# A decoder block on one NeuronCore: linear attention in chunks of 64 tokens, two to a tile, in smaller tiles of TensorE's array, with TensorE's step in another order

## The reference

```
h = layernorm(x);  q, k, v = split(h @ qkv_w.T + qkv_b)      # 16 heads of 16
q = relu(q) + 1e-6;  k = relu(k) + 1e-6
kv    = cumsum over tokens of (k outer v)                     # causal
num   = q . kv
den   = max(q . cumsum(k), 1e-6)
x     = x + (num / den) @ out_w.T + out_b
```

## Time and profile before

| | |
|---|---|
| runs | 379.93, 380.64, 380.88 us; median 380.64 |
| span of the profiled execution, first to last instruction | 377.9 us |
| TensorE busy | 356.6 us, 94% of the span |
| VectorE | 296.1 us, 78% |
| GpSimd | 279.1 us, 74% |
| ScalarE | 162.6 us, 43% |
| granted clock of TensorE, mean | 0.988 |
| the loop's score products, first and last | 31.0 and 271 us |

### The profile page before, as it was taken

How to read it: one execution, slowest core, us unless ns; L and a number is a source line. 1 busy time by engine, 2 the same in 40 slices (tenths; PEclk the granted TensorE clock), 3 DMA queues, 4 the chain that set the end, 5 groups by cost and what they waited for, 6 DMA issues and landing times. The chain is left out here.

```text
span 377.9 us, 10670 instructions
## 1 busy us (share of the span) xinstructions
PE 356.6 (94%) x3514; PEld 255.6 (68%) x3514; DVE 296.1 (78%) x922; ACT 162.6 (43%) x394; POOL 279.1 (74%) x414
## 2 busy tenths in 40 slices
PE   8999999999999999999999999999899989998781
PEld 4566677777677777767777777778676556655451
DVE  2588788898989898888898878886756588799462
ACT  2463553454455346436436524442456435331120
POOL 5338987766777866877867789898978888578455
PEclk9999999999999999999999999999999999999897
DMA  8993881200300120032121013003000233148750
GB/s 255 328 308 88 251 245 22 66 16 16 72 31 16 35 53 16 19 83 87 55 49 39 25 25 67 16 20 80 16 31 28 73 97 111 57 146 283 220 181 23
DMA packets 39309, 34.50 MB, mean 91 GB/s; under 512 B 4505, under 2 KB 38456, under 8 KB 39256
## 3 DMA queue, kind: packets, MB, share of 16 engines
q1 hardware_dynamic: 36392, 29.54, 27.7%
q0 software_dynamic: 1312, 3.37, 2.9%
q10 hardware_dynamic: 1552, 0.92, 0.9%
HBM read 17.55 MB, written 12.60 MB: 80 GB/s over the span
## 5 line engine op out<-in xcount | busy, mean ns | idle before, releaser
L1650 POOL TENSOR_TENSOR s_t<-s_t,causal 128x512 f32<-128x512 f32 x63 | 78.9, 1273 | 15.6 <-ACT s_t L961 15.4
L539 PE MATMUL bank<-h1t,w_qkv 128*128 128x512 f32 x112 | 52.9, 595 | 0.4 <-DVE x L1220 0.3
L1207 DVE TENSOR_TENSOR s_t<-sbank,causal 128x512 f32<-128x512 f32 x65 | 43.5, 671 | 1.1 <-PE sbank L560 1.0
L1642 POOL TENSOR_TENSOR state_wide<-state,own_pair 128x256 f32<-128x256 f32 x28 | 18.9, 676 | 25.5 <-DVE state L1198 24.4
L961 ACT ACTIVATE s_t<-sbank 128x512 f32<-128x512 f32 x63 | 33.7, 587 | 7.8 <-PE sbank L560 7.8
L560 PE MATMUL sbank<-arena 32*128 32x256 f32 x512 | 36.7, 400 | 0.0
L599 PE MATMUL bank<-s_t,vp 128*32 128x128 f32 x1024 | 34.6, 275 | 1.1 <-DVE s_t L1207 0.4
L546 PE MATMUL bank<-w_qkv,h1t 128*128 128x256 f32 x128 | 34.2, 389 | 0.0
L1658 POOL TENSOR_TENSOR rr<-ve,neg_half 128x3 f32<-128x3 f32 x36 | 31.9, 887 | 3.0
L684 PE MATMUL bank<-w_out,attn_t 128*128 128x256 f32 x128 | 33.6, 385 | 0.5 <-DVE attn_t L1288 0.5
L778 PE MATMUL sbank<-h1t,w 128*128 128x512 f32 x72 | 33.0, 596 | 0.5 <-ACT h1t L961 0.5
(11 more groups left out here) (231 smaller groups left out, 831.5 us busy)
## 6 DMA issues: line engine op xcount, KB each, us to landing
rden_t<-rden SPq DMA_DIRECT2D x64, 64.0 KB
rows<-x SPq DMA_DIRECT2D x32, 128.0 KB, 1.7
x<-in_x SPq DMA_DIRECT2D x7, 512.0 KB, 8.6
out<-x SPq DMA_DIRECT2D x7, 512.0 KB
we<-in_we SPq DMA_DIRECT2D x1, 2048.0 KB
xmask<-in_mask POOLq DMA_DIRECT2D x2, 616.0 KB, 10.3
rows<-empty SPq DMA_DIRECT2D x1, 1032.0 KB, 5.2
we<-in_we SPq DMA_DIRECT2D x1, 1024.0 KB
```

The costliest lines, as they stand in the source:

```text
L539: mm = pe.matmul(dst[:, :], w_qkv[:, ch, cb * P:(cb + 1) * P], h1t[:, g % 3, ch, :], start=(ch == 0), stop=(ch == CH - 1))
L1207: dve.tensor_tensor(s_t[:, r, :, :], sbank[r][:, :].rearrange("p (s q) -> p s q", s=4), causal[:, :].unsqueeze(1).to_broadcast([P, 4, P]), ...
L1650: pool.tensor_tensor(s_t[:, r, :, :], s_t[:, r, :, :], causal[:, :].unsqueeze(1).to_broadcast([P, 4, P]), ALU.mult)\
```

## The change

A tile now holds two chunks of 64 tokens. The scores of a chunk against itself are 64 by 64: for each of 2 channel blocks, 2 chunks and 4 head pairs one product in an array tile of 32 rows by 64 columns (16 products for 8). The numerators are products of 64 keys by 64 queries in tiles of 64 rows by 32 columns (32 for 16), into columns of sbank2 and 3 that the scores no longer use. There is a state per chunk: `inner_state` ahead of the tile's second chunk, `next_state` ahead of the next tile. `from_state` multiplies 64 queries of each chunk by its own state (16 products for 2, in column tiles of 32; 8 in a batch's first tile, which had none). The sums of keys by values are made per chunk (16 for 8), into sbank2 and 3. The masks are of 64 columns, and the whole score data is half as large: ScalarE copies it once, VectorE and GpSimd mask once each. The spread state is twice as large. s_t has two halves used in turn in the same room. `be_rest`, `over`, `past` and `block_oh` of the later expert stage share room with the spread state, which is no longer used then.

TensorE's step is reordered: transposes, q/k block, cross scores, from_state, numerators, sums, transposes of h1(F), values, denominators (now into bank 3), scores, and the rest as it was. The scores wait for more: `attn_ready` and all states of the tile. VectorE evicts the values and converts the mask later in its step, the attention product and the states come before the scan or query product, and the reciprocal of the softmax's sum stands between the two states. ScalarE's order is as it was. In the prologue VectorE makes `own_block` and `causal_ck` (three instructions for one). SP's program does not change.

The core of the diff (left out: declarations, the shared buffers, helper counts, the prologue; `own_pair`'s line):

```diff
-state = sb("state", [P, 3, CH, 2, HD])
...
+state = sb("state", [P, 3, 2, CH, 2 * HD])
+state_wide = sb("state_wide", [P, 2, 2, CH, RG, 2 * HD])
+own_block = sb("own_block", [P, RG, 2 * HD])
...
-sbank = [ctx.enter_context(nc.psum_tensor(f"sbank{i}", [P, 512], F32)) for i in range(RG)]
+sall = ctx.enter_context(nc.psum_tensor("sbank", [P, RG, 512], F32))
+sbank = [sall[:, r, :] for r in range(RG)]
...
+def part(t, c):
+    first = (t % GT) * P + c * CK
+    return slice(first, first + CK)
+def chunk(c):
+    return slice(c * CK, (c + 1) * CK)
...
-def updates(t):
-    return t - t // TPB
+def states(t):
+    return 2 * t - t // TPB
+def sums_of(c):
+    return sbank[2 + c][:, D + P:D + P + CH * 2 * HD]
...
-        wait(pe, s_masked, 2 * t)
-        wait(pe, s_copied, 2 * t)
+        wait(pe, s_masked, t)
+        wait(pe, s_copied, t)
+        wait(pe, attn_ready, t)
+        wait(pe, state_ready, states(t + 1))
         for ch in range(CH):
-            for r in range(RG):
...
+            for c in range(2):
+                for r in range(RG):
+                    rows = slice(32 * r, 32 * r + 32)
+                    both = sbank[r][chunk(c), 2 * ch * CK:2 * (ch + 1) * CK].rearrange("p (s n) -> p s n", s=2)
+                    mm = pe.matmul(both, kt(slot, ch)[rows, part(t, c)], qpair(slot, ch)[rows, :, part(t, c)],
+                                   start=True, stop=True)
         mm.then_inc(s_done, 1)
     def denominators(g):
         wait(pe, qkc_ready, 2 * g + 2)
         wait(pe, den_ready, g)
-        wait(pe, ktok_ready, GT * g + 1)
-        wait(pe, v_ready, GT * g + 2)
+        wait(pe, h1t_ready, min(GT * g + AHEAD + 1, NT))
+        wait(pe, x2_ready, GT * g - 3)
         for ch in range(CH):
             for j in range(GT):
-                mm = pe.matmul(bank[2][32 * j:32 * j + 32, D:D + P], to_heads[:, ch, :],
+                mm = pe.matmul(bank[3][32 * j:32 * j + 32, D:D + P], to_heads[:, ch, :],
                                qkc(g % 2, ch)[:, tok(j)], start=(ch == 0), stop=(ch == CH - 1),
...
     def from_state(t):
         slot = (t // GT) % 2
-        wait(pe, h1t_ready, min(t + 1 + AHEAD + 1, NT))
...
+        wait(pe, s_copied, on_act(t + 1))
+        wait(pe, s_masked, on_dve(t + (t == NT - 1)))
+        wait(pe, wide_ready, t + 1)
+        for c in range(1 if starts(t) else 0, 2):
+            for ch in range(CH):
+                for r in range(RG):
+                    at = D + ch * CK
+                    pe.matmul(sbank[2 + c][32 * r:32 * r + 32, at:at + CK], state_wide[:, t % 2, c, ch, r, :],
+                              qall(slot, ch)[:, part(t, c)], start=(ch == 0), stop=False, skip_group_check=True)
     def numerators(t):
-        wait(pe, h1t_ready, min(t + 1 + AHEAD + 1, NT))
-        wait(pe, x2_ready, t - 2)
         first = starts(t)
...
         for ch in range(CH):
             for par in range(2):
+                for c in range(2):
+                    for r in range(RG):
+                        head = HC * ch + 2 * r + par
+                        at = D + ch * CK
+                        v_of = vp[chunk(c), t % 3, head // 2, 32 * par:32 * par + 32]
+                        mm = pe.matmul(sbank[2 + c][32 * r:32 * r + 32, at:at + CK], v_of,
+                                       s_t[chunk(c), t % 2, r, 2 * ch + par, :],
+                                       start=(first and c + ch + par == 0),
+                                       stop=(ch + par == 2), skip_group_check=True)
+        mm.then_inc(num_done, 1)
+    def key_values(t):
+        wait(pe, ktok_ready, t + 1)
+        wait(pe, v_ready, t + 1)
+        wait(pe, s_copied, on_act(t))
+        for ch in range(CH):
+            for c in range(2 if (t + 1) % TPB else 1):
                 for r in range(RG):
-                    head = HC * ch + 2 * r + par
...
+                    v_of = vp[chunk(c), t % 3, RG * ch + r, :].rearrange("p (q e) -> p q e", q=4)[:, 0:4:3, :]
+                    mm = pe.matmul(sums_of(c)[32 * r:32 * r + 32, ch * 2 * HD:(ch + 1) * 2 * HD],
+                                   k_tok[chunk(c), t % 2, ch * P + 32 * r:ch * P + 32 * r + 32], v_of,
+                                   start=True, stop=True, skip_group_check=True)
+        mm.then_inc(st_done, 1)
     def step(pe, i):
         K, M, B, F, V = i, i - 1, i - 3, i + AHEAD, i + 1
...
         if is_tile(K):
             wait(pe, qk_ready, 4 * (K // GT) + 2)
             wait(pe, ktok_ready, K)
-            wait(pe, den_ready, -(-K // GT))
             wait(pe, v_ready, K + 1)
             for ch in range(CH):
                 mm = transpose(bank[2][:, ch * P:(ch + 1) * P], kt((K // GT) % 2, ch)[:, tok(K)])
             qk_block(g, i % GT, bank[0])
         if i > NT:
             gate_products(pe, i - NT - 1, 0)
-        if is_tile(F):
...
         if is_tile(B):
             wait(pe, h2t_ready, B + 1)
             off = (B // TPB) * KX
                 mm = pe.matmul(bank[1][:, 0:KX], h2t[:, B % 2, ch, :], w_score[:, ch, off:off + KX],
                                start=(ch == 0), stop=(ch == CH - 1))
             mm.then_inc(sc_done, 1)
-        if is_tile(V):
...
         if i == NT - 1:
...
             centre_w3(pe)
         if is_tile(M):
+            from_state(M)
             numerators(M)
-        if is_tile(K) and (K + 1) % TPB:
...
         if i == 0:
             pe.wait_ge(prep_act, 7)
             pe.wait_ge(prep_dve, 5)
+        if is_tile(K):
+            key_values(K)
+        if i > NT:
+            gate_products(pe, i - NT - 1, 1)
+        if is_tile(F):
+            wait(pe, x2_ready, i - 3)
+            tr_h1(F, bank[3])
+        if is_tile(V):
+            wait(pe, ktok_ready, K + 1)
+            values(V)
+        if is_tile(K) and K % GT == 0:
+            denominators(K // GT)
         if is_tile(K):
             scores(K)
         if is_tile(B):
...
             mm.then_inc(out_done, 1)
         if is_tile(B):
             wait(pe, pt_ready, B + 1)
-            if is_tile(M):
-                wait(pe, attn_ready, M + 1)
+            wait(pe, x2_ready, B)
+            wait(pe, h1t_ready, min(i + AHEAD + 1, NT))
             if is_tile(K):
-                wait(pe, state_ready, 2 * updates(K + 1))
+                wait(pe, den_ready, K // GT + 1)
             pe.matmul(bank[3][:, 0:D], prob_t[:, B % 2, :], w_value[0:KX, B // TPB, :], start=True, stop=True)\
                 .then_inc(px_done, 1)
         if i >= NT:
...
         K, M, B, F = i, i - 1, i - 3, i + AHEAD
         g, blk = i // GT + 1, i % GT
         if is_tile(M):
-            for r in range(on_act(M + 1) - on_act(M)):
+            if on_act(M + 1) > on_act(M):
                 wait(act, s_done, M + 1)
-                wait(act, num_done, M)
-                copy(flat(s_t[:, r, :, :]), sbank[r][:, :]).then_inc(s_copied, 1)
+                wait(act, num_done, M - 1)
+                copy(s_t[:, M % 2, 2:RG, :, :].rearrange("p r a n -> p r (a n)"), sall[:, 2:RG, 0:4 * CK])\
+                    .then_inc(s_copied, 1)
         if is_tile(B):
             wait(act, t2_done, B + 1)
...
         wait(dve, den_done, g - 1)
         dve.tensor_tensor(qkc(g % 2, ch), ksum(g % 2, ch), qall(g % 2, ch), ALU.mult).then_inc(qkc_ready, 1)
-    def new_state(t):
...
+    def inner_state(t):
+        wait(dve, st_done, t + 1)
+        wait(dve, wide_ready, t - 1)
+        wait(dve, state_ready, states(t))
+        now = state[:, t % 3, 1, :, :].rearrange("p c e -> p (c e)")
+        if starts(t):
+            dve.tensor_copy(now, sums_of(0)).then_inc(state_ready, 1)
+        else:
+            dve.tensor_tensor(now, sums_of(0), state[:, t % 3, 0, :, :].rearrange("p c e -> p (c e)"), ALU.add)\
+                .then_inc(state_ready, 1)
+    def next_state(t):
+        wait(dve, state_ready, states(t) + 1)
+        wait(dve, wide_ready, t - 1)
+        dve.tensor_tensor(state[:, (t + 1) % 3, 0, :, :].rearrange("p c e -> p (c e)"), sums_of(1),
+                          state[:, t % 3, 1, :, :].rearrange("p c e -> p (c e)"), ALU.add).then_inc(state_ready, 1)
+    def mask_scores(t, r):
+        wait(dve, s_done, t + 1)
+        wait(dve, num_done, t - 1)
+        dve.tensor_tensor(s_t[:, t % 2, r:r + 2, :, :],
+                          sall[:, r:r + 2, 0:4 * CK].rearrange("p r (a n) -> p r a n", a=4),
+                          causal_ck[:, :].unsqueeze(1).unsqueeze(1).to_broadcast([P, 2, 4, CK]), ALU.mult)\
+            .then_inc(s_masked, 1)
     def step(dve, i):
         K, M, X1, B, X2, V, L = i, i - 1, i - 2, i - 3, i - 4, i + 1, i + AHEAD + 1
         g = i // GT + 1
         if is_tile(M):
-            mask_scores(M, 0, 1 if i < NT else RG)
+            mask_scores(M, 0)
+            if i == NT:
+                mask_scores(M, 2)
         if is_tile(X1):
             wait(dve, out_done, X1 + 1)
             wait(dve, x_biased, X1 + 1)
             last.then_inc(mv_ready, 1)
         if g < NG:
             qk_evict(4 * g + i % GT, bank[0])
```

(47 more changed lines are left out.)

124 lines of the change are left out of this document (18 added, 106 removed).

## The result

The kernel after takes **407.6 us** (median of 5 runs, 406.2 to 415.8) where the kernel before, on the same chip, took 380.9 (379.9 to 382.9): 1.0705 times as long, interval 1.0645 to 1.0765. So +26.7 us, where +9.7 was predicted; the time lies outside the range. Run again unedited beside the first experiments it took 409.0, 1.076 [1.068, 1.085]. The first profile (span 414.0 us) had four stretches at half clock inside the loop; the second (span 408.3) had one, so timelines are taken from the second.

What follows compares the result with a forecast made beforehand. TensorE was taken to bound the loop, with a new chain of waits after the change. Steps 3 to 23 +11.2 and +1.1, steps 0 to 2 -1.0, steps 24 to 31 -2.0, prologue +0.4: +9.7, so 390.3 us, range 376 to 405.

Steps and rivals of the forecast that it cites:

- the chain of waits: Moved h1 transposes, eviction, parities, exp, reciprocal, next_state, scores, then VectorE's route to x1: +2.4 us per group of four steps.
- the place of the stall: TensorE idle before the scores' weight loads, waiting for VectorE's state, 1.5 us in a group's third and fourth step.
- TensorE's own work, 7.30 a step: TensorE's parts summed from first transpose to the next: 7.30 us a step where it was 7.91.
- The second rival: Two row groups don't run side by side on TensorE: numerators take 0.87 us, about 407 us in all; chance 0.08.
- The scan, 1.50: VectorE's scan in the third step's chain, taken as 1.50 us from a mean of 1.62 with overlapped ends off.
- the spread is covered: GpSimd's spread of the inner state, ready at about 5 in the frame, has until 2.57 of the next step.
- No h1 tile: Steps 24 to 31: next_state's wait mostly covered by TensorE's work, 0.25 of 0.6 kept on average, -2.0 us.
- Supply of instructions, 0: TensorE's short records issue fast enough at 0.0075 us each, so the sum holds no cost for issue.
- issue sets the pace: Rival: TensorE's records cost 0.040 us each by issue, not streaming; about 500 us in all; chance 0.02.
- the third and fourth step: Steps of a group with parity products ahead of the exp: 9.22 and 9.4 us by the chain.
- the prediction's frame: Predicted TensorE step timed from its first transpose: scores from 5.18, end 7.30; exp ends at 6.31 in half the steps.
- The first rival: TensorE's saving is kept, 0.6 us a step over 31 steps: 362 us; break-even 0.56 a step shorter chain; chance 0.14.

Runs made afterwards that it cites:

- before_split_all: Kernel before, with from_state in 32 records for 4 and numerators and scores also cut to 64 queries each, about 170 records a step for 95: 394.8 us.
- exp_state_early: Kernel after, with ScalarE's exp ahead of the h1t eviction and parity products and TensorE's from_state ahead of the q/k block: 385.7 us.
- before_split_state: Kernel before, with only from_state cut into 32 records for 4: 379.5 us.
- early_half: exp_state_early with from_state in two column tiles of 64, 16 records for 32: 385.0 us.
- scan_half: Kernel after, with exp ahead of h1t eviction and parities, scan and first query product ahead of the attention product, from_state in 16 records: 391.2 us.
- exp_pool: Kernel after, with exp ahead of h1t eviction and parities, and GpSimd's mask ahead of the state spread: 420.7 us.

## Why the prediction was wrong

The direction, the chain of waits and the place of the stall were right. The size was not, +9.7 for +26.7, and four terms of the sum failed; against the profiled span 20.7 us are missing (+30.4 for +9.7). By the figures below, terms 1, 2 and 4 make about 10, 5 and 6 of them, an estimate, since they meet in the same steps.

1. **TensorE's own work, 7.30 a step: 7.62 to 7.7.** Measured from start to start: cross scores 0.49 (0.41 predicted), from_state 0.59 (0.53), numerators 0.66 (0.49), sums 0.39, at times 0.66 (0.35), h1 transposes 0.27 (0.22); scores 0.63 was right, and the q/k block too (1.72, but 1.82 behind a wait). Each part behind a change of shape starts 0.05 to 0.1 later than I reckoned. The numerators' 64 records start within 0.64 us, 10 ns apart on average, where I took 6.7: most follow each other at 6 to 7 ns, as the 16 in the earlier trace rows did, but with pauses of about 30 to 55 ns between runs of them, and many in the second half are 11 or 16 ns apart. I carried the price of a short part over to one four times as long. 0.3 a step on 31 steps is 10 us, and it enters in full, since the stalls are counted from TensorE's work. The second rival had this place and the right time, 407, but not the cause: the tiles do run eight side by side (0.66 for 64 records; four side by side would be 16 rounds of 0.054, 0.87).
2. **The scan, 1.50: 2.09.** "mean 1.62, overlapped ends off" was the wrong choice. After the change inner_state releases GpSimd's spread just as VectorE comes to the scan. The second step of a group is 8.57 for 7.94, most of it by this; the q/k block waits for x1 there. Nine scans of the second run have the spread beside them; they take 1.68 to 2.25 us, 5.4 in all above the 1.50 that I took. I had written that the spread is covered; its own end is, but not what it does to its neighbour.
3. **"No h1 tile" in steps 24 to 31, -2.0: +6.1.** The seven steps take 7.60, 7.69, 7.69, 6.93, 6.49, 6.49 and 6.70 us in the kernel before and 7.71, 8.58, 8.54, 8.54, 6.89, 8.44 and 6.97 after. More than half of the +6.1 is term 4: TensorE runs dry twice in the middle of the sums, for 3.3 us together.

```profile
277.69 0.26 PE L637 MATMUL sbank<-vp,k_tok 64*32 64x32 f32 x5 [1.51 <-issue]
...
293.39 0.27 PE L637 MATMUL sbank<-vp,k_tok 64*32 64x32 f32 x8 [1.80 <-issue]
```

   The first three steps still hold a q/k block. The second and third of them wait 0.43 us for x1 ahead of it, the first and second 0.34 and 0.16 for the state ahead of the scores: there the way from x1 over q/k block, numerators and sums to the state and the next x1 is longer than TensorE's work. I had asked only about the exp there.
4. **Supply of instructions, 0.** The rival "issue sets the pace" got 0.02 because 16 records kept up at 7.5 ns each. As a steady pace it is indeed wrong. As a reserve that runs out it costs 6.0 us of waits in the loop of the kernel after (6.7 in the first profile, where two of them, 1.51 and 1.80 us, are each followed by a stretch at the lower clock level). before_split_all shows what more records alone can cost, 14 us with 6.4 of such waits.

Right were the third and fourth step (9.39 and 9.29 for 9.22 and 9.4), no stall for the state at a batch's last tile, and the scores' saving. The third step is in part luck: the h1 transposes start 3.95 us after the q/k block and not 3.50 (term 1), while the scan there, with no spread beside it, takes 1.28 and not 1.50. The exp's end in the prediction's frame is 6.38 by its own terms, not 6.31; nothing hangs on it. The first rival's break-even, a chain shorter by 0.56 a step, was tested by exp_state_early (0.58 shorter): it comes to 385.7 and not to 362, because TensorE's own work is 8.03 in that order. No version tried beats the kernel before; before_split_state, at 0.997, is 0.3% off, about the smallest difference that these runs tell. The 5 us left over in early_half were not taken apart by cause, only by place: tiles 0 to 3 take 23.0 us for 20.9, tiles 3 to 24 170.5 for 169.1, and 24 to 31 51.2 for 49.6.

The Trainium skill, TensorEngine Tiling (Array Packing), section "Key Properties", says that a change of tiling mode drains TensorE. The runs agree that a change costs time, 0.07 to 0.13 us in a part beside it; the drain itself no run here shows.

## What to carry to other kernels

Smaller array tiles save streaming but multiply records and changes of shape: price a part by records at its own length, add 0.1 us for each change of shape (what it was here), and put parts of one shape next to each other. When TensorE's order is moved, follow the loop of waits that closes over a step (here x1 to x1), not only the new wait: removing the visible stall of 16 us gave 7. Work that needs nothing new belongs ahead of the wait, as from_state here: the edit was worth 16 us, part of it by spacing the short records. And count records: TensorE can run out of instructions though their steady pace looks free.

## What the runs showed of the hardware

- **VectorE's scan and GpSimd's spread take turns.** The two in exp_state_early, in the second and third step of one group:

```profile
170.97 1.26 POOL L1673 TENSOR_TENSOR state_wide<-state,own_block 128x512 f32<-128x512 f32 x1 [0.17 <-DVE state L1217]
179.26 2.19 POOL L1673 TENSOR_TENSOR state_wide<-state,own_block 128x512 f32<-128x512 f32 x1
```

```profile
171.06 2.25 DVE L1200 TENSOR_TENSOR_SCAN arena<-arena,zero 128x512 f32<-128x512 f32 x1
179.10 1.28 DVE L1200 TENSOR_TENSOR_SCAN arena<-arena,zero 128x512 f32<-128x512 f32 x1
```

  The one that starts first keeps its 1.27 us, the one that starts 0.1 or 0.2 us behind takes 2.2: it pays for nearly all of the other. Where the spread began earlier, less was paid: 2.09 us for the scan at 0.26 us behind it and 1.68 at 0.66, in the second run of the kernel after. The Trainium skill, GPSIMD Engine Reference, section "Specifications", says that the two contend where VectorE has two inputs in SBUF, as the scan has here. The trace agrees.
- **Instructions come in packets** of 16 KB, and TensorE can run dry, mostly in or just behind a part of short records: for 0.3 to 2.3 us, and for 3.6, 4.4 and 5.5 us (before_split_all, scan_half, exp_pool) where the expert weights are loading at 320 GB/s and more. It goes on 1.2 to 1.6 us after the next packet has landed.
- **A dry spell can cost twice.** In exp_state_early 1.84 us without instructions (57.2 to 59.2) are followed by a q/k block of 3.5 us for 1.82, at granted clock 0.51, 1.2 GHz:

```profile
59.23 0.27 PE L546 MATMUL bank<-ident,h 128*128 128x128 f32 x1 [1.84 <-issue]
...
60.29 3.67 PE L558 MATMUL bank<-h1t,w_qkv 128*128 128x512 f32 x4
```

```profile
60.29:63.80 3.51, 3.51 (x11) 1.51 (x6) 0.00 (x0) 0.39 (x2) 2.58 (x6) 0.51 0.02 5
```
